# Two post-norm layers on one core: feature blocks through DRAM in whole rows, an expert tile in quarters, two evictions moved

## The chip, the core and the metric

The kernel runs on one core of a Trainium2 chip. The time is device microseconds of a whole execution: three runs gave 1348.04, 1350.30 and 1350.33 us, so the median is 1350.3 us. TensorE does matmuls and transposes, VectorE (DVE), ScalarE (ACT) and GpSimd (POOL) do the elementwise work, and SyncE (SP) issues most DMAs. Every engine runs its own list of instructions in order; semaphores tie the lists together.

## The reference, cut to what matters

```python
x = _layernorm(x + _L0_attn_ref(x, Wq, bq, Wk, bk, Wv, bv, gamma))      # layer A, attention
x = _layernorm(x + _L0_ffn_ref(x, gate_w, gate_b, expert_w, expert_b))  # 8 experts, gated
x = _layernorm(x + _L1_attn_ref(x, Wqkv, Wproj, bproj))                 # layer B, attention
x = _layernorm(x + _L1_ffn_ref(x, w_router, w_block))                   # top 75% of tokens

def _L1_attn_ref(x, Wqkv, Wproj, bproj):          # x: 8 batches of 1024 tokens, 256 features
    qkv = jnp.einsum('bnm,fm->bnf', x, Wqkv).reshape(b, n, 16, 48)
    q, k, v = (qkv[..., :16], qkv[..., 16:32], qkv[..., 32:])
    attn = jax.nn.softmax(jnp.einsum('bnhd,bngd->bnhg', q, k) / 8.0, axis=-1)
    out = jnp.einsum('bnhg,bngd->bnhd', attn, v).reshape(b, n, -1)
    return jnp.einsum('bni,mi->bnm', out, Wproj) + bproj
```

Layer B's attention is over the 16 heads of one token, not over tokens: for every token a 16 by 16 matrix of scores.

## The kernel before, in words

Each of the 8 batches goes through three stages: its layer-A attention, its experts, its layer-B attention with the last block. `turn(a, b, c)` interleaves three batches: attention A of `a`, experts of `b`, layer B of `c`. The order of each engine's instructions is written out by hand in that engine's `turn`; `closing` and `ending` do the same for the last two batches. The layer-B heads of a batch `c` are computed in six calls of `turn` and one of `closing`, seven places with the same order of work; those of the last batch come in `ending`, where little else is left to interleave.

**Through DRAM.** The projection to q, k and v gives six blocks of 128 features by 1024 tokens (`b_f`, feature tiles ft 0 to 5: two for q, two for k, two for v). Each is stored by one DMA of 512 KB to `scratch_qkv` from one of four slots (two halves of `stage`, `part`, and `flat_we` in the last batch), and a slot is written again only when its earlier store has landed. q, k and v are then read back in another layout, in which a partition holds one coordinate r (an eighth of the tokens) and one dimension d, and the heads and tokens run along the row: eight DMAs of 128 KB for each, one for each r, into 16 partitions each (`home_rows`), in pieces of 512 bytes. q and v go to `ct`, k to `keys`. In the last batch SP and ACT issue four q loads each, and SP five and POOL three k loads. The output of the heads is stored in the same manner (`o_store`, eight DMAs of 128 KB, four by SP in `b_loado` and four by ACT in `b_storeo`) and read back into `bt` by two DMAs of 512 KB.

**The heads.** `b_turnq` (ACT) and `b_turnv` (POOL, L705) re-order what was loaded: `blockdiag` is then built from it by the spreads. A spread is one instruction over 128 by 2048 fp16 elements that multiplies by a mask; DVE (L1554) and ACT (L873) share them. Eight DVE spreads make the first half of `blockdiag` for q, without which the score matmuls `S0` can't start. TensorE computes the scores in four blocks S0 to S3 (96 matmuls with 16 moving columns each), transposes the softmax (PT0 to PT3) and computes the outputs O0 to O3. These use two PSUM banks in turn: S3 waits until DVE has read S2, O0 until PT2 is read, O1 until PT3 is read, O2 until O0 is read. The outputs are evicted by ACT (high half) and DVE (low half) into `stage`, which held the turned v; so ACT's first output eviction waits for all v spreads.

**The experts.** An expert tile is 128 tokens; `a_moe(b, t)` on TensorE is four quarters of six matmuls, 128x512 each, one for each of four PSUM banks. DVE chains two quarters onto `x1`, ACT scales the other two into `part`, and POOL's `a_sum` adds them up (L670, L673, L677), reading two SBUF operands each. Tiles 1 to 7 are spread over the turn.

In POOL's list `b_turnv(c, 0)` stands right behind `a_sum(b, 0)` and ahead of `a_sum(b, 1)`. SP's `b_loadv` waits until both `b_turnq` are done, because v is loaded over q.

Of the kernel before, what the change touches and what calls it, by code (L numbers as in the profile page):

```python
# [5 lines left out]
def build_two_layer_postln(nc, x, wqk_t, bqk, wv, bv, gamma, gate_w, gate_b, expert_w, expert_b,  # L6
# [9 lines left out]
    NB, C, D = x.shape  # L16
# [28 lines left out]
    with ctx:  # L45
# [166 lines left out]
        k_rest = sem("k_rest")  # L212
# [10 lines left out]
        o_stored = sem("o_stored")  # L223
# [140 lines left out]
        K_SP = 5  # L364
# [20 lines left out]
        def o_store(r):  # L385

            return (scratch_o[:, :, r, :].rearrange("h d n -> d h n"),
                    ohl[DH * r:DH * (r + 1), :, :, :].rearrange("p h l n -> p h (l n)"))

# [6 lines left out]
        def home_rows(home, r):  # L396
            return home[DH * r:DH * (r + 1), :].rearrange("p (h n) -> p h n", h=H)
# [26 lines left out]
        class StepCount:  # L424
# [4 lines left out]
            def next(self, n):  # L429
# [8 lines left out]
        q_src, k_src, v_src = [scratch_qkv[D * n:D * (n + 1)].rearrange("(h d) (r n) -> h d r n", d=DH, r=T)  # L438
                               for n in range(3)]
# [19 lines left out]
        def _(sp):  # L459
# [33 lines left out]
            def b_f(b, k):  # L493
# [10 lines left out]
                sp.dma_start(scratch_qkv[P * ft:P * (ft + 1)], slots[s]).then_inc(stored[s], 16)  # L504

            def b_flast(b, ft):

                for k in range(12):
                    if f_tile(b, k)[0] == ft:
                        name = turn_of(b, f"F{k}")  # L510
                        sp.wait_ge(b_free[b_ring(name)], b_read(b, name))
                        sp.sem_inc(waits_held, 1)
                s = f_slot(b, ft)
                sp.dma_start(scratch_qkv[P * ft:P * (ft + 1)], slots[s]).then_inc(stored[s], 16)

            def b_loadq(b):
                for ft in (0, 1):
                    sp.wait_ge(*f_stored(b, ft))
                    sp.sem_inc(waits_held, 1)
                if b == NB - 1:  # L520
                    for r in range(T // 2):
                        sp.dma_start(home_rows(q_home(b), r), q_src[:, :, r, :].rearrange("h d n -> d h n"))\
                            .then_inc(q_loaded, 16)
                    return
                if later(b):
                    sp.wait_ge(ff_full, 4 * b)
                for r in range(T):
                    sp.dma_start(home_rows(q_home(b), r), q_src[:, :, r, :].rearrange("h d n -> d h n")).then_inc(q_loaded, 16)

            def b_loads(b):  # L530
                for ft in (0, 1, 3, 2):
                    b_flast(b, ft)
                b_loadq(b)
                b_loadk(b)
                sp.wait_ge(k_loaded, 16 * (T * b + K_SP))
                sp.sem_inc(waits_held, 1)
                sp.wait_ge(k_rest, 16 * (T - K_SP))
# [5 lines left out]
            def b_loadk(b):  # L543
                for ft in (2, 3):
                    sp.wait_ge(*f_stored(b, ft))
                    sp.sem_inc(waits_held, 1)
# [6 lines left out]

                for r in range(K_SP if b == NB - 1 else T):
                    sp.dma_start(keys[DH * r:DH * (r + 1), :, :],
                                 k_src[:, :, r, :].rearrange("h d n -> d h n")).then_inc(k_loaded, 16)

            def b_loadv(b):
                for ft in (4, 5):
                    sp.wait_ge(*f_stored(b, ft))  # L560
                    sp.sem_inc(waits_held, 1)
# [4 lines left out]
                for r in range(T):  # L566
                    sp.dma_start(home_rows(v_home(b), r), v_src[:, :, r, :]).then_inc(v_loaded, 16)

            def b_loado(b):
# [4 lines left out]
                for r in range(T // 2):  # L574
                    sp.dma_start(*o_store(r)).then_inc(o_stored, 16)
                sp.wait_ge(o_stored, 128 * (b + 1))
                sp.sem_inc(waits_held, 1)
# [1931 lines left out]
```

## Time and profile before

| | us |
|---|---|
| median of 3 runs | 1350.3 |
| profiled execution | 1349.4 |
| its span, first to last instruction | 1347.6 |
| TensorE busy | 1167.3 (87%) |
| DVE busy | 937.1 (70%) |
| ACT busy | 722.6 (54%) |
| POOL busy | 571.8 (42%) |
| mean granted TensorE clock | 0.891 |

Busy matmul time counts pipelined matmuls with modelled ends. A wait is shown as idle time before an instruction, in brackets, with what released it. "SPq" and "ACTq" are the sequencers that issue DMAs. Times in the timeline are counted from the first instruction.

### The profile page before, as it was taken

The numbers are of one execution on the slowest core, as the hardware profiler recorded it, in microseconds if no ns is written. First come the engines' busy times: TensorE is split into PE (matmuls) and PEld (weight loads), VectorE is DVE, ScalarE is ACT, GpSimd is POOL, SyncE is SP. The second block draws the span as 40 slices with busy tenths as digits, with TensorE's granted clock in tenths as the row PEclk, the third lists the DMA queues.
The fourth block names the chain that finished last, engine by engine and source line by source line (L and its number), as shares of the span: only waits on it lengthen the run. The fifth ranks groups of instructions, "written<-read, shape, count | busy, mean of one in ns | idle before, by whom it ended". The sixth has DMA issues, their size and how long they took to land.

```text
span 1347.6 us, 31178 instructions
## 1 busy us (share of the span) xinstructions
PE 1167.3 (87%) x12264; PEld 748.0 (56%) x12264; DVE 937.1 (70%) x2124; ACT 722.6 (54%) x1145; POOL 571.8 (42%) x882
## 2 busy tenths in 40 slices
PE   6688899998989999998999989898999988897464
PEld 4444466655665546655566556655566555654452
DVE  3544578677775868767775778668686777755866
ACT  3223375347753575547853477545754477544653
POOL 2235435335354355245354355354462352551124
PEclk8689898799979998799988999799987998799557
DMA  5000092203902075201902056021932029026430
GB/s 188 16 1 16 18 166 23 80 9 101 127 2 79 17 167 54 66 15 68 168 2 80 9 115 113 17 64 33 174 31 64 1 87 133 2 64 114 75 96 32
DMA packets 94009, 90.64 MB, mean 67 GB/s; under 512 B 7110, under 2 KB 83144, under 8 KB 93608
## 3 DMA queue, kind: packets, MB, share of 16 engines
q1 hardware_dynamic: 82008, 77.24, 29.3%
q0 software_dynamic: 2064, 6.69, 1.6%
q10 hardware_dynamic: 9792, 4.72, 1.4%
q8 instruction: 98, 1.61, 0.5%
q14 instruction: 47, 0.39, 0.1%
HBM read 46.68 MB, written 41.94 MB: 66 GB/s over the span
## 4 chain that ended last, share of the span: by engine, by line
PE 57%; DVE 18%; DMA 7%; issue 6%; ACT 5%; POOL 4%; ACTq 1%; SPq 1%; DVEq 0%; POOLq 0%
PE bank L1994 54%; DVE keys L1640 2%; DVE stats L1384 2%; DMA bt<-scratch_o 2%; DVE x L1525 2%; DVE gelu L1642 2%; POOL rs L655 2%; DMA scratch_o<-stage 2%; PE bank L2004 1%; ACT x L996 1%; DVE ct L1353 1%; DMA keys<-scratch_qkv 1%; ACTq L966 1%; ACT part L873 1%; DVE x L1708 1%
## 5 line engine op out<-in xcount | busy, mean ns | idle before, releaser
L1994 PE MATMUL bank<-we,at 128*128 128x512 f16 x1536 | 373.7, 403 | 1.9 <-DVE x L1525 1.9
L1994 PEld LDWEIGHTS bank<-we,at 128*128 128x128 f16 x1536 | 154.4, 102 | 194.6 <-issue 41.6
L670 POOL TENSOR_TENSOR part<-part 128x512 f32<-128x512 f32 x64 | 84.2, 1316 | 276.5 <-ACTq L1022 276.5
L873 ACT ACTIVATE part<-bank,wexp 128x256 f32<-128x256 f32 x256 | 104.3, 470 | 159.6 <-PE bank L1994 102.9
L1525 DVE SCALAR_TENSOR_TENSOR x<-bank,wexp,x 128x256 f32<-128x256 f32 x256 | 122.7, 479 | 53.0 <-PE bank L1994 46.5
L1994 PE MATMUL bank<-bt,wqkv 128*128 128x512 f16 x576 | 137.3, 380 | 20.8 <-DVE stage L1353 12.3
L996 ACT ACTIVATE x<-x,nm,rs 128x256 f32<-128x256 f32 x184 | 100.3, 593 | 69.3 <-POOL nm L658 68.1
L1353 DVE TENSOR_TENSOR stage<-bank,stage 128x512 f16<-128x512 f32 x110 | 74.4, 686 | 82.5 <-ACT stage L873 82.2
L651 POOL TENSOR_SCALAR nm<-mv 128x2 f32<-128x2 f32 x128 | 33.4, 261 | 207.1 <-DVE mv L1389 201.5
L1994 PE MATMUL bank<-keys,blockdiag 128*128 128x16 f16 x3072 | 97.5, 193 | 21.8 <-DVE blockdiag L1554 10.0
L1994 PEld LDWEIGHTS bank<-keys,blockdiag 128*128 128x128 f16 x3072 | 96.1, 103 | 26.4 <-issue 14.5
L873 ACT ACTIVATE stage<-bank 128x512 f16<-128x512 f32 x110 | 64.9, 597 | 77.2 <-PE bank L1994 75.5
L655 POOL TENSOR_TENSOR rs<-ve,half 128x2 f32<-128x2 f32 x128 | 96.0, 750 | 10.7
L1994 PEld LDWEIGHTS bank<-bt,wqkv 128*128 128x128 f16 x576 | 52.1, 97 | 86.1 <-DVE stage L1353 21.8
L2004 PE MATMUL bank<-const,x 128*128 128x128 f32 x384 | 59.4, 284 | 35.8 <-ACT x L996 25.5
L1994 PE MATMUL bank<-xs,blockdiag 128*128 128x16 f16 x2688 | 72.9, 173 | 16.8 <-issue 16.7
L1994 PEld LDWEIGHTS bank<-xs,blockdiag 128*128 128x128 f16 x2688 | 71.9, 102 | 18.9 <-issue 18.8
L873 ACT ACTIVATE blockdiag<-stage,const 128x2048 f16<-128x2048 f16 x40 | 78.1, 1993 | 0.0
L705 POOL COPY stage<-ct 128x2048 f16<-128x2048 f16 x14 | 54.2, 3871 | 49.4 <-DMA ct<-scratch_qkv 49.4
L1384 DVE BATCH_NORM_STATS2 stats<-x 128x6 f32<-128x256 f32 x184 | 68.9, 416 | 7.9 <-POOL x L677 4.4
L2004 PEld LDWEIGHTS bank<-const,x 128*128 128x128 f32 x384 | 45.5, 145 | 51.9 <-ACT x L996 33.2
L873 ACT ACTIVATE at<-bank 128x512 f16<-128x512 f32 x64 | 38.2, 596 | 62.4 <-PE bank L2004 60.9
(212 smaller groups left out, 2275.4 us busy)
## 6 DMA issues: line engine op xcount, KB each, us to landing
scratch_qkv<-stage SPq DMA_DIRECT2D x39, 512.0 KB, 3.3
ct<-scratch_qkv SPq DMA_DIRECT2D x112, 128.0 KB, 6.5
x_in<-in_x_dram SPq DMA_DIRECT2D x32, 256.0 KB, 2.7
bt<-scratch_o SPq DMA_DIRECT2D x16, 512.0 KB, 4.1
keys<-scratch_qkv SPq DMA_DIRECT2D x61, 128.0 KB, 6.0
out_dram<-x POOLq DMA_DIRECT2D x24, 256.0 KB, 2.7
scratch_qkv<-part SPq DMA_DIRECT2D x8, 512.0 KB, 7.8
scratch_o<-stage SPq DMA_DIRECT2D x32, 128.0 KB, 3.5
```

Of the source, the lines that this page charges most:

```text
L651: pool.tensor_scalar(nm[side][:, k, :], mv[side][:, k, :, 0], -1.0, None, ALU.mult)
L655: pool.tensor_tensor(rs[side][:, k, :], ve[side][:, k, :], half[:, 0:2], ALU.pow)\
L670: pool.tensor_tensor(part[:, 0:2, :], part[:, 0:2, :], part[:, 2:4, :], ALU.add)\
L705: pool.tensor_copy(v_rows[hf].rearrange("p (s c) h -> p s c h", c=8), turned(v_home(b), hf)).then_inc(v_turned[hf], 1)
L873: return act.activation(dst, src, ACT.Copy, scale=scale)
L996: ins = act.activation(dsts[t], srcs[t], ACT.Identity, bias=nm[side][:, k, t:t + 1], scale=rs[side][:, k, t:t + 1])
L1353: return dve.tensor_tensor(dst, src, hi, ALU.subtract)
L1384: ins = dve.bn_stats(stats[side][:, t, :], srcs[t])
L1525: ins = dve.scalar_tensor_tensor(out=dst, in0=m_bank[q][:, D * (e % 2):D * (e % 2 + 1)], scalar=wexp[:, t, e:e + 1], in1=dst, op0=ALU.mult ...
L1640: dve.tensor_scalar(beats_on(b)[:, o:o + P * (T - 1 - t)], scores_of(b)[:, P * (t + 1):C], me, None, ALU.is_le, ALU.add, accum_out=rowsum[ ...
L1994: ins = pe.matmul(dst, lhs, rhs, start=(n == 0), stop=(n == len(terms) - 1))
L2004: ins = pe.transpose(ps[:, 2 * P * k + P * t:2 * P * k + P * (t + 1)], src[:, 2 * p + t, P * k:P * (k + 1)], ident)
```

## The change

1. **Layout in DRAM.** The order of the features is permuted by the host in `Wqkv` (`by_dim` for q and k, `by_head` for v) and in `Wproj`, so that a block of 128 features holds, for each r, a whole row of each partition of the layout that is wanted. A block is now stored in pieces of 512 bytes (eight for each partition, `by_feature`) and loaded by one DMA of 512 KB with 4 KB for each of 128 partitions. So q, k and v take two loads each in place of eight, all issued by SP. The head outputs are stored by two DMAs of 512 KB in rows of 4 KB, and read back by two in pieces of 512 bytes; each read waits only for its own store. ACT issues no DMA any more, and POOL no k load.
2. **Order of the loads of the last batch.** The first q block is loaded before the store of block 2 is waited for; k's blocks are loaded 3 first.
3. **Expert tile 3 in quarters.** Its first quarter goes ahead of S3, two behind it, and the last between PT2 and PT3.
4. **ACT and DVE around the outputs.** Evictions O0 and O1 go ahead of ACT's part of expert tile 3. ACT's eviction of PT2 goes ahead of a layer-norm step. One v spread moves from ACT to DVE, which evicts PT2 before the first two spreads of half 1.

```diff
+        def half_of(home, ft):
+            return home[:, 2 * C * (ft % 2):2 * C * (ft % 2 + 1)]
+        def by_feature(memory):
+            return memory.rearrange("a m -> (a m)").rearrange("(r p n) -> p r n", r=T, p=P)
...
-                sp.dma_start(scratch_qkv[P * ft:P * (ft + 1)], slots[s]).then_inc(stored[s], 16)
+                sp.dma_start(by_feature(qkv_block(ft)), slots[s].rearrange("p (r n) -> p r n", r=T)).then_inc(stored[s], 16)
...
+            def load_block(b, ft, home, loaded):
+                sp.wait_ge(*f_stored(b, ft))
+                sp.sem_inc(waits_held, 1)
+                sp.dma_start(half_of(home, ft), qkv_block(ft)).then_inc(loaded, 16)
...
             def b_loads(b):
-                for ft in (0, 1, 3, 2):
+                for ft in (0, 1, 3):
                     b_flast(b, ft)
-                b_loadq(b)
+                load_block(b, 0, q_home(b), q_loaded)
+                b_flast(b, 2)
+                load_block(b, 1, q_home(b), q_loaded)
                 b_loadk(b)
...
             def b_loadv(b):
...
-                for r in range(T):
-                    sp.dma_start(home_rows(v_home(b), r), v_src[:, :, r, :]).then_inc(v_loaded, 16)
+                for ft in (4, 5):
+                    load_block(b, ft, v_home(b), v_loaded)
 
             def b_loado(b):
...
-                for r in range(T // 2):
-                    sp.dma_start(*o_store(r)).then_inc(o_stored, 16)
-                sp.wait_ge(o_stored, 128 * (b + 1))
-                sp.sem_inc(waits_held, 1)
                 for ht in range(KD):
-                    sp.dma_start(bt[:, ht, :, :].rearrange("p l n -> p (l n)"),
-                                 scratch_o[8 * ht:8 * ht + 8].rearrange("h d r n -> (h d) (r n)"))\
-                        .then_inc(o_loaded, 16)
+                    sp.dma_start(scratch_o[P * ht:P * (ht + 1)], ohl[:, 8 * ht:8 * ht + 8, :, :].rearrange("p h l n -> p (h l n)"))\
+                        .then_inc(o_stored[ht], 16)
+                for ht in range(KD):
+                    sp.wait_ge(o_stored[ht], 16 * (b + 1))
+                    sp.sem_inc(waits_held, 1)
+                    sp.dma_start(bt[:, ht, :, :].rearrange("p l n -> p (l n)").rearrange("p (r n) -> p r n", r=T),
+                                 by_feature(scratch_o[P * ht:P * (ht + 1)])).then_inc(o_loaded, 16)
...
             def turn(a, b, c):
...
-                    b_spreadv(c, 1, range(6, T))
-                if b is not None:
-                    a_moe(b, 3)
-                if c is not None:
+                    b_spreadv(c, 1, range(7, T))
                     b_o(c, 0)
                     b_o(c, 1)
+                if b is not None:
+                    a_moe(b, 3)
+                if c is not None:
                     b_o(c, 2)
                     b_o(c, 3)
```

On TensorE, the heads of one batch in a turn, from expert tile 1 to the output matmuls (`keys,blockdiag` is a score block, `const,prob` its transpose, `we,at` an expert tile, `xs,blockdiag` the outputs). Before:

```order
L1994 MATMUL bank<-we,at 128x512 x24
L1994 MATMUL bank<-keys,blockdiag 128x16 x192
L1994 MATMUL bank<-we,at 128x512 x24
L2169 MATMUL bank<-const,prob 128x128 x4
L1994 MATMUL bank<-keys,blockdiag 128x16 x96
L2169 MATMUL bank<-const,prob 128x128 x4
L1994 MATMUL bank<-keys,blockdiag 128x16 x96
L1994 MATMUL bank<-we,at 128x512 x24
L2169 MATMUL bank<-const,prob 128x128 x8
L1994 MATMUL bank<-xs,blockdiag 128x16 x384
```

And after, from the transposition PT0 on:

```order
L2128 MATMUL bank<-const,prob 128x128 x4
L1955 MATMUL bank<-keys,blockdiag 128x16 x96
L2128 MATMUL bank<-const,prob 128x128 x4
L1955 MATMUL bank<-we,at 128x512 x6
L1955 MATMUL bank<-keys,blockdiag 128x16 x96
L1955 MATMUL bank<-we,at 128x512 x12
L2128 MATMUL bank<-const,prob 128x128 x4
L1955 MATMUL bank<-we,at 128x512 x6
L2128 MATMUL bank<-const,prob 128x128 x4
L1955 MATMUL bank<-xs,blockdiag 128x16 x384
```

The 24 matmuls of expert tile 3 stood in one piece between S3 and PT2; six now stand ahead of S3, twelve behind it and six between the two transpositions.

On SP, the DMAs of one turn from the first stores of a batch on (`ct` takes q, later v). Before:

```order
L504 DMA scratch_qkv<-stage 128x2048 x3
L528 DMA ct<-scratch_qkv 16x16x256 x8
L504 DMA scratch_qkv<-part 128x2048
L504 DMA scratch_qkv<-stage 128x2048 x2
L555 DMA keys<-scratch_qkv 16x16x256 x8
L567 DMA ct<-scratch_qkv 16x16x256 x8
L575 DMA scratch_o<-stage 16x16x256 x4
L579 DMA bt<-scratch_o 128x2048 x2
L469 DMA x_in<-in_x_dram 128x2x256 x4
```

After:

```order
L503 DMA scratch_qkv<-stage 128x8x256 x3
L518 DMA ct<-scratch_qkv 128x2048 x2
L503 DMA scratch_qkv<-part 128x8x256
L503 DMA scratch_qkv<-stage 128x8x256 x2
L518 DMA keys<-scratch_qkv 128x2048 x2
L518 DMA ct<-scratch_qkv 128x2048 x2
L563 DMA scratch_o<-stage 128x2048 x2
L568 DMA bt<-scratch_o 128x8x256 x2
L468 DMA x_in<-in_x_dram 128x2x256 x4
```

The order is the same; twenty-four loads from `scratch_qkv` became six, over all 128 partitions each.

On ACT, from the end of the v spreads of half 0 to the output evictions (`xs<-bank` evicts a transposition, `blockdiag<-stage` is a spread, `x<-x,nm,rs` a layer-norm step, `part<-bank` the expert part, `stage<-bank` an output). Before:

```order
L873 ACTIVATE blockdiag<-stage,const 128x128x16 x2
L996 ACTIVATE x<-x,nm,rs 128x256 x2
L873 ACTIVATE xs<-bank 128x512 x2
L873 ACTIVATE blockdiag<-stage,const 128x128x16 x2
L873 ACTIVATE part<-bank,wexp 128x256 x4
L873 ACTIVATE stage<-bank 128x16x8x4 x4
L873 ACTIVATE at<-bank 128x2x256
L966 DMA scratch_o<-stage 16x16x256 x4
```

After:

```order
L851 ACTIVATE blockdiag<-stage,const 128x128x16 x2
L851 ACTIVATE xs<-bank 128x512
L967 ACTIVATE x<-x,nm,rs 128x256 x2
L851 ACTIVATE xs<-bank 128x512
L851 ACTIVATE blockdiag<-stage,const 128x128x16
L851 ACTIVATE stage<-bank 128x16x8x4 x2
L851 ACTIVATE part<-bank,wexp 128x256 x4
L851 ACTIVATE stage<-bank 128x16x8x4 x2
```

The expert part moved behind two output evictions, one spread left for DVE, and the four DMA issues are gone.

## Rows read from the trace of the kernel before

**Rows 1.** The page: TensorE's and other engines' busy time; the last chain.

```profile
PE 1167.3 (87%) x12264; PEld 748.0 (56%) x12264; DVE 937.1 (70%) x2124; ACT 722.6 (54%) x1145; POOL 571.8 (42%) x882
...
PE 57%; DVE 18%; DMA 7%; issue 6%; ACT 5%; POOL 4%; ACTq 1%; SPq 1%; DVEq 0%; POOLq 0%
```

**Rows 2.** Timeline, a turn: start us, us, engine, what, count, [idle before <-releaser].

```profile
508.79 6.34 SPq L567 DMA_DIRECT2D ct<-scratch_qkv  x8
...
510.13 7.36 DVE L1554 TENSOR_SCALAR blockdiag<-prob,const 128x2048 f16<-128x2048 f16 x8
...
513.24 1.05 POOL L677 TENSOR_TENSOR x<-x,part 128x256 f32<-128x256 f32 x1
...
517.41 2.73 DVE L1554 TENSOR_SCALAR blockdiag<-shared,const 128x2048 f16<-128x2048 f16 x4
...
518.54 4.59 PE L1994 MATMUL bank<-keys,blockdiag 128*128 128x16 f16 x144
...
522.53 3.74 POOL L705 COPY stage<-ct 128x2048 f16<-128x2048 f16 x1 [8.24 <-DMA ct<-scratch_qkv]
```

**Rows 3.** Timeline of the last such place, in closing.

```profile
1137.77 4.40 PE L1994 MATMUL bank<-keys,blockdiag 128*128 128x16 f16 x138 [0.92 <-issue]
```

**Rows 4.** By line, ns min/median/max: DVE's q spreads, POOL's v turns; timeline of one.

```profile
L1554 DVE TENSOR_SCALAR blockdiag<-prob,const x56: 737/744/1767, 198.0 to 1136.9; 128x2048 f16<-128x2048 f16 x56
...
L705 POOL COPY stage<-ct x14: 3735/3822/4436, 210.2 to 1151.2; 128x2048 f16<-128x2048 f16 x14
...
829.20 2.73 DVE L1554 TENSOR_SCALAR blockdiag<-shared,const 128x2048 f16<-128x2048 f16 x4
...
831.23 4.44 POOL L705 COPY stage<-ct 128x2048 f16<-128x2048 f16 x1 [5.15 <-DMA ct<-scratch_qkv]
```

**Rows 5.** DMA issues (count, KB, median us to landing); windows (last: DMA share, GB/s).

```profile
ct<-scratch_qkv SPq DMA_DIRECT2D x112, 128.0 KB, 6.5
...
bt<-scratch_o SPq DMA_DIRECT2D x16, 512.0 KB, 4.1
...
scratch_o<-stage SPq DMA_DIRECT2D x32, 128.0 KB, 3.5
...
510.20:513.00 2.80, 2.80 (x38) 2.51 (x35) 2.80 (x3) 2.48 (x3) 2.69 (x2) 1.00 1.28 118
...
570.00:573.00 3.00, 3.00 (x15) 1.17 (x13) 1.79 (x4) 0.84 (x2) 2.68 (x3) 1.00 0.94 340
```

**Rows 6.** Timeline, S3 to O3, PE, ACT and DVE apart; one window (PEclk 0.50).

```profile
537.26 3.04 PE L1994 MATMUL bank<-keys,blockdiag 128*128 128x16 f16 x96 [0.68 <-DVE prob L1588]
540.13 6.42 PE L1994 MATMUL bank<-we,at 128*128 128x512 f16 x24
...
548.49 5.03 PE L1994 MATMUL bank<-xs,blockdiag 128*128 128x16 f16 x192 [1.07 <-issue]
554.99 5.27 PE L1994 MATMUL bank<-xs,blockdiag 128*128 128x16 f16 x192 [1.47 <-issue]
...
551.83 1.54 ACT L873 ACTIVATE part<-bank,wexp 128x256 f32<-128x256 f32 x4
...
548.91 2.73 DVE L1554 TENSOR_SCALAR blockdiag<-stage,const 128x2048 f16<-128x2048 f16 x4
...
540.10:541.00 0.90, 0.90 (x10) 0.35 (x7) 0.67 (x1) 0.05 (x1) 0.62 (x1) 0.50 0.06 18
```

**Rows 7.** Waits: who, for whom, us in total, times, longest.

```profile
PE bank L1994 <- DMA bt<-scratch_o: 11.0, 5, 8.3
```

**Rows 8.** Timeline of the last batch: q, scores, v, outputs.

```profile
1243.82 2.42 DVE L1567 COPY we<-at 128x2048 f16<-128x2048 f16 x1 [3.97 <-DMA at<-scratch_qkv]
...
1251.92 4.26 PE L1994 MATMUL bank<-keys,blockdiag 128*128 128x16 f16 x134 [10.01 <-DVE blockdiag L1554]
...
1267.72 3.83 ACT L873 ACTIVATE stage<-xs 128x2048 f16<-128x2048 f16 x1 [4.69 <-DMA xs<-scratch_qkv]
...
1304.80 1.46 PE L1994 MATMUL bank<-wproj,bt 128*128 128x256 f16 x6 [8.33 <-DMA bt<-scratch_o]
```

## What the change was predicted to do

> **What bounds the kernel now.** First the page: TensorE is busy for 87% of the span and holds 57% of the chain that ended last, DVE 18% [rows 1]. So a microsecond by which TensorE's list is held up counts in full, and one saved elsewhere counts only where TensorE waits for it. Second, the timeline of one turn around the place where TensorE could start the scores: S0 starts at 518.54, straight behind expert tile 1, and the eight DVE spreads that it needs ended at 510.13 + 7.36 = 517.49 [rows 2]. That is a slack of 1.05 us, and the reader should keep it in mind. This place comes seven times with the same order, six in turns and one in closing, where TensorE already waits 0.92 us before S0 [rows 3]. Third, the same turn from S3 to O3, where TensorE waits 0.68, 1.07 and 1.47 us [rows 6]. Fourth, the last batch, where nothing covers its DMAs: TensorE waits 10.01 us ahead of S0 and 8.33 us ahead of the projection, ACT 4.69 us for v [rows 8].
>
> **Part 1, loads over 128 partitions.** Before, v is issued at 508.79 and POOL gets it at 522.5, after 8.24 us of waiting [rows 2]: 1 MB in eight DMAs into 16 partitions each, at 118 GB/s with the DMA share at 1.28. Two DMAs of 512 KB over 128 partitions are in the trace as the read of `bt`: 4.1 us to landing, and 340 GB/s in its stretch [rows 5]. By that row both v blocks have landed some 5 us after the issue, near 514. The Trainium skill explains the two rates (SBUF — State Buffer, "Door 1: The DMA port swizzle"): bandwidth depends on how many of 16 ports the partitions reach, and 16 neighbouring ones reach four. That changes no term here; it says that the row of `bt` is the one to go by.
>
> What does the early v buy? Nothing on TensorE, which doesn't wait for it, and it has a price. POOL's list has `b_turnv(c, 0)` right behind `a_sum(b, 0)`, which ends at 513.24 + 1.05 = 514.29 [rows 2]. So POOL starts its 3.74 us copy of v there, in the middle of the eight spreads, where it used to start behind all twelve. Do the two engines disturb each other? A spread takes 0.74 us at the median, but 1.77 at most [rows 4]; the slow ones lie beside `a_sum`, and so eight take 7.36 us where four others take 2.73 [rows 2]. The other way round, the copy that began at 831.23, while the last of four spreads from 829.20 was running, took 4.44 us where the shortest take 3.74, longer by what that spread still had to run, 0.70 [rows 4]. So they take turns. The nearest row for the sum: four spreads are done at about 514.8, POOL's copy then runs to 518.6, and the four that are left take 4 x 0.66 = 2.65, to 521.2. S0 starts at 521.3 in place of 518.54: **2.75 us lost in each of six turns**. In closing there is no slack, so the whole 3.74 is lost. Sum: 6 x 2.75 + 3.74 = **+20.2 us**. It doesn't matter when exactly v lands: any time up to the last of the eight spreads, 8.7 us after the issue, gives the same loss. Bounds: nothing (if the copy, which reads one operand, holds DVE back less than `a_sum` does) and 7 x 3.74 = 26. I take the value worked out, since 831.23 shows this very copy and this very spread exclude each other.
>
> By the Trainium skill (SBUF — State Buffer, "SBUF: two separate sides") DVE and GpSimd share one pair of SBUF ports, and whichever starts first keeps it for its whole instruction while the other stands still. By that rule the earlier v costs the 20 us above; if POOL merely waited for DVE and never the reverse, it would cost none. The rule speaks against the change, and the rows of the spreads and the copy agree with it.
>
> S1, tile 2 and PT0 are behind S0 on TensorE and move with it. DVE falls back by 3.7 us, but catches up: its reading of S0 and S1 had waits for ACT and TensorE between. q and k also land earlier, which nobody waits for in a turn.
>
> **Stores in 512-byte pieces.** No row shows a 512 KB store in such pieces. The nearest is the outputs' store, also in 512-byte pieces, 128 KB in 3.5 us; the nearest of the size is the read of `bt`, 512 KB in 4.1 us [rows 5]. So a store takes between about 4 us and, if four times the size took four times as long, 14. I take 4.5, nearer to the row of the size, because most of the 3.5 us for 128 KB must be latency. ACT's eviction F4 waits for the store of block 0, with several evictions and layer-norm steps of both engines between, which cover 4.5 us; near the upper end it would cost several microseconds a turn, and that counts under slower still.
>
> **Outputs through DRAM.** TensorE waits 11.0 us in five places for `bt`, 8.3 of them in the last batch [rows 7]; the other 2.7 lie in the turns. SP now issues two stores where eight on two queues were needed, and the first read waits for its own store alone. The read in 512-byte pieces lies between the 340 and the 118 GB/s of rows 5: 3.1 to 8.9 us for 1 MB; I take 4. That gives **-2.7 us**, bounded by 0 and, at 8.9, by 2 us lost in each turn.
>
> **Part 2, the last batch.** DVE waits 3.97 us for q before its 2.42 us turn, then spreads, and S0 follows at 1251.92 [rows 8]. With q over 128 partitions, two loads at the rate of `bt`, it lands before DVE is free at 1243.82 - 3.97 = 1239.85: S0 4.0 us sooner, and k isn't late either, with two loads in place of eight. v then no longer holds ACT for 4.69 us [rows 8]; behind it stands the exponential of score block 2, for which DVE waits; DVE has work of its own for about half of that time, so I count 2.1 more, an estimate. The fifth spread on DVE delays O2 by about 1.1 there. Behind the outputs ACT issues no DMAs ahead of its next step and the 8.33 us wait shrinks; DVE, still busy with the batch before, bounds the gain, and I take a quarter of the wait, 2.1. Sum: -4.0 - 2.1 + 1.1 - 2.1 = **-7.1 us**, bounds -10 and -3.
>
> **Parts 3 and 4.** The first quarter of tile 3 fills the 0.68 us ahead of S3. At PEclk 0.50, which is 1.2 GHz and what the stretch shows [rows 6], six matmuls of 512 columns take 2.56 us, at 2.4 GHz 1.28. So S3 ends 0.6 to 1.9 us later than before. From there DVE's list is the limit: it reads S3, spreads, reads PT2 and PT3 and spreads again, now five times in place of four (2.73 / 4 = +0.68). Against that, ACT's expert part of 1.54 us no longer stands ahead of the eviction of O0, which ends the 1.47 us wait ahead of O2 [rows 6]. Late 1.3 to 2.6, early 1.5 to 2: **0 us**, give or take 1 us in each of seven places.
>
> **Sum.** 1349.4 + 20.2 - 2.7 - 7.1 + 0 = 1359.8 for an execution like the profiled one; the median of the three runs lies 0.9 above that, so **1360.7**, or 0.8% slower.
>
> **Rivals.** *Faster: the copy doesn't hold DVE back* (or v lands after the last of the eight spreads, over 8.7 us from its issue). Then only the gains stay: 1350.3 - 9.8 = 1340.5, own range 1333 to 1348. For it: no row shows DVE's spread waiting for this copy, only the copy for the spread. Against it: the spreads beside `a_sum`. *Slower still: the clock or the 512-byte reads.* If most of tile 3 runs at 1.2 GHz once it is split by S3, PT3 comes 2 us late and O2 with it, 7 x 2 = 14 us on top: 1375. The same size comes if `bt` is read at 118 GB/s. For it: six matmuls at the low clock ahead of S3; against it: what clock there is afterwards comes back sooner too. *The change doesn't do what it says:* loads stay at 118 GB/s, because it is their pieces' source in DRAM and not the 16 partitions that limits them. Then no collision and little gain: 1349.
>
> **How the numbers follow.** The forecast has 0.67, the first rival 0.18, slower still 0.10, unchanged loads 0.05. About 0.2% (2.7 us) is what a measurement of this kernel can tell from no change. The forecast's own range, 1352 to 1369, comes from the bounds of parts 3 and 4 (7 us) and of the rest (3 us); a little of it lies within 0.2% or below. Faster: 0.17 + 0.03 = 0.20; same: 0.04 + 0.04 + 0.01 = 0.09; slower: 0.71. The range of 8 in 10 reaches from 1338, which takes in over half of the first rival, to 1370.
>
> **What would show it.** In the profile after: v landed some 5 us from its issue; POOL's copy starting right behind the first `a_sum`, one DVE spread of about 4.4 us in each turn, and S0 with 2.7 us of idle TensorE ahead of it, released by DVE. In the last batch, S0's wait near 6 us, and none of ACT for v. Ahead of O2 a wait near 1.5 us, released by ACT behind DVE's spreads. The prediction is wrong if spreads stay under 1.8 us, and then the time is near 1340.

## The result, and the profile after

The changed kernel takes **1357.9 us** at the median of seven runs (1353.3 to 1361.4); the kernel before took 1347.1 beside it. The ratio is 1.0072, with a 95% interval of 1.0053 to 1.0091: slower by 0.7%. Measured again (run e10 below) it was 1.0040, 1.0022 to 1.0057. The forecast was 1360.7 us and slower.

The page of the kernel after, as [rows 1]: busy time and the chain that ended last.

```profile
span 1359.6 us, 30973 instructions
...
PE 1169.8 (86%) x12264; PEld 750.2 (55%) x12264; DVE 977.3 (72%) x2132; ACT 707.0 (52%) x1137; POOL 577.5 (42%) x879
...
PE 54%; DVE 26%; issue 7%; ACT 6%; POOL 5%; DMA 2%; DVEq 0%; SPq 0%; POOLq 0%; ACTq 0%
```

Three things are to be seen. DVE's busy time grew by 40 us, though it got only one more spread a batch, 6 us in all; the rest is spreads that take longer, as shown below. Its share of the chain rose from 18% to 26%. The DMAs' share of the chain fell from 7% to 2%. The span less TensorE's busy time, the **idle time of TensorE**, was 1347.6 - 1167.3 = 180.3 us before and is 189.8 now, 9.5 more. I use this number for every run below, since it doesn't contain how fast the matmuls themselves ran. It is read from one execution of each kernel; the kernel after, profiled again, gave 187.8.

The same turn as in [rows 2], timeline of the kernel after:

```profile
515.93 1.39 SPq L518 DMA_DIRECT2D ct<-scratch_qkv  x2
517.24 10.86 DVE L1515 TENSOR_SCALAR blockdiag<-prob,const 128x2048 f16<-128x2048 f16 x8
520.33 1.05 POOL L666 TENSOR_TENSOR x<-x,part 128x256 f32<-128x256 f32 x1
521.58 3.97 POOL L694 COPY stage<-ct 128x2048 f16<-128x2048 f16 x1 [0.20 <-DMA ct<-scratch_qkv]
528.02 4.22 DVE L1515 TENSOR_SCALAR blockdiag<-shared,const 128x2048 f16<-128x2048 f16 x4
528.20 6.02 PE L1955 MATMUL bank<-keys,blockdiag 128*128 128x16 f16 x192 [2.39 <-issue]
```

POOL, done with the first sum at 521.38, waits 0.20 us for v and starts its copy at 521.58, 5.65 us after v's issue at 515.93 (before, it was 13.7 us). That is in the middle of the eight spreads. These take 10.86 us in place of 7.36, and S0 has 2.39 us of idle TensorE ahead of it. The profile names no releaser for that wait ("issue"), but the last of the eight spreads ends at 528.10, 0.10 before S0 starts. The wait is 2.39 or 2.40 us in each of the six turns. POOL's part of the next sum now lies beside the four spreads of half 1, which take 4.22 in place of 2.73; that was not in the prediction. All spreads of q, ns min/median/max, as in [rows 4]:

```profile
L1515 DVE TENSOR_SCALAR blockdiag<-prob,const x56: 740/1210/4257, 200.6 to 1154.9; 128x2048 f16<-128x2048 f16 x56
```

Seven of the 56, one in each place, take 4.2 us. Closing, to be read against [rows 3], and the last batch, against [rows 8]:

```profile
1143.75 5.35 PE L1955 MATMUL bank<-we,at 128*128 128x512 f16 x24 [1.88 <-DVE x L1486]
1144.88 11.27 DVE L1515 TENSOR_SCALAR blockdiag<-prob,const 128x2048 f16<-128x2048 f16 x8
1147.30 4.17 POOL L694 COPY stage<-ct 128x2048 f16<-128x2048 f16 x1
...
1156.25 3.93 PE L1955 MATMUL bank<-keys,blockdiag 128*128 128x16 f16 x123 [7.15 <-issue]
...
1256.61 2.47 DVE L1528 COPY we<-at 128x2048 f16<-128x2048 f16 x1
...
1264.60 6.02 PE L1955 MATMUL bank<-keys,blockdiag 128*128 128x16 f16 x192 [6.21 <-issue]
...
1275.76 3.81 ACT L851 ACTIVATE stage<-xs 128x2048 f16<-128x2048 f16 x1
...
1314.02 1.46 PE L1955 MATMUL bank<-wproj,bt 128*128 128x256 f16 x6 [6.23 <-DMA bt<-scratch_o]
```

DVE's turn of q has no wait any more (3.97 before), S0 waits 6.21 (10.01), ACT doesn't wait for v (4.69), the projection waits 6.23 (8.33). The projection's is now the only wait of TensorE for `bt`: those in the turns are gone. What closing shows is taken up in the part on why the prediction was right.

### The profile page after: what moved, and what is told of

Same layout as the page of the kernel before. It is cut to its first block, busy times and chain, and to the rows that moved or that the text cites. A ratio compares the mean times of both kernels' runs of the same rounds, so it can differ in the third digit from the quotient of the medians.

```text
span 1359.6 us, 30973 instructions
## 1 busy us (share of the span) xinstructions
PE 1169.8 (86%) x12264; PEld 750.2 (55%) x12264; DVE 977.3 (72%) x2132; ACT 707.0 (52%) x1137; POOL 577.5 (42%) x879
## 3 DMA queue, kind: packets, MB, share of 16 engines
q1 hardware_dynamic: 89544, 82.35, 19.2%
## 4 chain that ended last, share of the span: by engine, by line
PE 54%; DVE 26%; issue 7%; ACT 6%; POOL 5%; DMA 2%; DVEq 0%; SPq 0%; POOLq 0%; ACTq 0%
PE bank L1955 51%; DVE blockdiag L1515 5%; DVE x L1486 3%; DVE keys L1601 2%; DVE stats L1345 2%; PE bank L1965 2%; DVE gelu L1603 2%; POOL rs L644 2%; ACT x L967 1%; DVE ct L1314 1%; ACT part L851 1%; DVE x L1669 1%; DVE gt L1400 1%; DMA out_dram<-x 1%; DVE prob L1549 1%
## 5 line engine op out<-in xcount | busy, mean ns | idle before, releaser
L659 POOL TENSOR_TENSOR part<-part 128x512 f32<-128x512 f32 x64 | 87.5, 1367 | 297.0 <-ACTq L993 297.0
L926 ACT ACTIVATE prob<-prob 128x512 f32<-128x512 f32 x32 | 20.2, 630 | 130.0 <-DVE prob L1549 130.0
L700 POOL TENSOR_TENSOR prob<-prob,srec 128x512 f32<-128x512 f32 x32 | 36.6, 1144 | 99.8 <-DVE srec L1557 99.8
L1515 DVE TENSOR_SCALAR blockdiag<-prob,const 128x2048 f16<-128x2048 f16 x56 | 76.4, 1435 | 1.0
L1515 DVE TENSOR_SCALAR blockdiag<-stage,const 128x2048 f16<-128x2048 f16 x96 | 76.5, 845 | 0.0
```

The costliest lines, as they stand in the source:

```text
L659: pool.tensor_tensor(part[:, 0:2, :], part[:, 0:2, :], part[:, 2:4, :], ALU.add)\
L700: pool.tensor_tensor(pr, pr, srec[:, q % 2, :, None].broadcast_to([P, 32, H]), ALU.mult)\
L1515: ins = dve.tensor_scalar(blockdiag[:, dst_half, :, DH * r:DH * (r + 1)], rows, mask[:, r:r + 1], None, ALU.mult)
```

## Experiments

Each ratio is against the kernel before, run on the same chip beside it, with its 95% interval. "Idle" is TensorE's idle time in the profiled execution (180.3 before, 189.8 after).

| | ratio | idle, us |
|---|---|---|
| after | 1.0072 (1.0053 to 1.0091) | 189.8 |
| e10, after, measured again | 1.0040 (1.0022 to 1.0057) | 187.8 |
| e1, after, copy moved | 0.9883 (0.9858 to 0.9909) | 170.6 |
| e2, after, copy made twice | 1.0245 (1.0218 to 1.0272) | 221.5 |
| e3, layout alone | 1.0020 (1.0006 to 1.0034) | 189.6 |
| e4, layout alone, copy moved | 0.9869 (0.9844 to 0.9894) | 169.9 |
| e5, before, copy moved | 1.0007 (0.9976 to 1.0039) | 183.2 |
| e6, before, outputs alone | 0.9955 (0.9936 to 0.9974) | 177.6 |
| e7, e1 without quarters | 0.9894 (0.9863 to 0.9924) | 169.8 |
| e8, e1 without part 4 | 0.9912 (0.9883 to 0.9940) | 175.4 |
| e9, after, copy waits for 8 spreads | 1.0030 (1.0013 to 1.0047) | 183.7 |
| e11, after without quarters | 1.0036 (1.0014 to 1.0059) | 189.5 |
| e12, before, with a collision put in | 1.0262 (1.0229 to 1.0295) | 216.2 |

### e1 and e2: take the cause away, double it

e1, in POOL's `turn` and `closing` (the `if` lines of `turn` are left out):

```diff
                 a_sum(b, 0)
-                b_turnv(c, 0)
                 a_sum(b, 1)
+                b_turnv(c, 0)
```

> The kernel after, with POOL's copy of v for half 0 moved behind the sum of expert tile 1 (in the turn and in closing), so that it can't start before TensorE has done that tile. Theory (the copy stands between DVE's eight spreads and holds up S0): the 2.4 us of idle TensorE ahead of S0 is gone in six turns (14.4 us), and closing gets 3.7 back, so 1357.9 - 18 = about 1340 us, no DVE spread over 1.8 us. Rival 1 (the wait ahead of S0 is made up for later, since DVE and ACT bound the stretch behind it): the gap goes, but it comes back ahead of S2, PT0 or S3, and the time is 1350 to 1358. Rival 2 (the loss against the kernel before comes from the stores and reads in 512-byte pieces or from the order of expert tile 3): 1358 us.

Measured: 1335.7 us, 1.17% below the kernel before, some 4 us less than expected. The theory holds: TensorE's idle time fell by 189.8 - 170.6 = 19.2 us, and the longest DVE spread of q takes 1.77 us. e1's turn, timeline:

```profile
508.67 7.36 DVE L1514 TENSOR_SCALAR blockdiag<-prob,const 128x2048 f16<-128x2048 f16 x8
...
517.08 6.06 PE L1954 MATMUL bank<-keys,blockdiag 128*128 128x16 f16 x192
...
521.51 0.69 DVE L1548 TENSOR_TENSOR prob<-bank,smax 128x512 f32<-128x512 f32 x1
521.72 3.75 POOL L694 COPY stage<-ct 128x2048 f16<-128x2048 f16 x1
...
522.90 0.69 DVE L1554 TENSOR_REDUCE ssum<-prob 128x32 f32<-128x512 f32 x1 [0.70 <-ACT prob L925]
...
525.94 0.69 DVE L1554 TENSOR_REDUCE ssum<-prob 128x32 f32<-128x512 f32 x1 [0.70 <-ACT prob L925]
```

The eight spreads take 7.36 us again, as before, and no wait stands ahead of S0 in any of the six turns. The copy, from 521.72 to 525.47, now lies beside DVE's softmax in f32, and there nobody is held: the copy takes 3.75 us, and the same sum over `prob` takes 0.69 beside the copy (at 522.90) and after its end (at 525.94). So it is not "POOL beside DVE" that costs, but POOL beside the fp16 spreads. By the Trainium skill (SBUF — State Buffer, "SBUF: two separate sides") only certain DVE instructions take the pair of ports that DVE shares with GpSimd: those in a 2-port perf mode, and those with two SBUF inputs while GpSimd reads SBUF too. The rows agree in so far as the spreads are held and these f32 steps are not; which mode an instruction runs in, they don't show.

e2, in `b_turnv`:

```diff
+                if hf == 0:
+                    pool.tensor_copy(v_rows[hf].rearrange("p (s c) h -> p s c h", c=8),
+                                     turned(v_home(b), hf)).then_inc(v_again, 1)
+                    pool.wait_ge(v_again, b + 1)
                 pool.tensor_copy(v_rows[hf].rearrange("p (s c) h -> p s c h", c=8),
                                  turned(v_home(b), hf)).then_inc(v_turned[hf], 1)
```

> The kernel after, with POOL's copy of v for half 0 made twice in a row at the same place (the same data, so the result is unchanged). Theory: the second copy also gets between the eight spreads, and costs S0 another 3.7 us in each of seven places, 26 us, so about 1384 us, with two DVE spreads of over 4 us in each turn or one of 8. Rival 1: DVE gets all of its spreads done between the two copies, or only one copy can catch it: 1358 to 1362 us. Rival 2, the copy doesn't matter: 1358 us.

Measured: 1382.1 us, 24 more than the kernel after; expected 26. That the two numbers are so near is in part chance: the idle time grew by 31.7 us, not 26, and TensorE's busy time in the profiled execution was 11.3 us shorter (1158.5 against 1169.8), for which I have no reason. Timeline of e2 (from the third spread on):

```profile
524.84 13.38 DVE L1520 TENSOR_SCALAR blockdiag<-prob,const 128x2048 f16<-128x2048 f16 x6
...
526.59 4.24 POOL L696 COPY stage<-ct 128x2048 f16<-128x2048 f16 x1
530.88 3.99 POOL L699 COPY stage<-ct 128x2048 f16<-128x2048 f16 x1
...
538.32 5.98 PE L1960 MATMUL bank<-keys,blockdiag 128*128 128x16 f16 x192 [7.27 <-issue]
```

S0's wait grew from 2.39 to 7.27 us. Both copies get in between, with spreads between them: two of the eight take over 4 us here (4.27 and 4.12).

### e3 to e6: the layout, with and without the collision

e3 undoes parts 3 and 4; e4 is e3 with e1's edit. The diff shows TensorE's list and the main lines of ACT's; the `if` lines, and the order around PT2 on ACT and DVE, are left out.

```diff
-                    a_moe(b, 3, (0,))
                     b_s(c, 3)
-                    a_moe(b, 3, (1, 2))
+                    a_moe(b, 3)
                     b_pt(c, 2)
-                    a_moe(b, 3, (3,))
                     b_pt(c, 3)
...
-                    b_spreadv(c, 1, range(7, T))
-                    b_o(c, 0)
-                    b_o(c, 1)
+                    b_spreadv(c, 1, range(6, T))
                     a_moe(b, 3)
+                    b_o(c, 0)
+                    b_o(c, 1)
```

> The kernel after with parts 3 and 4 undone: expert tile 3 in one piece behind S3, ACT's expert part ahead of the output evictions, its layer-norm step ahead of PT2, six spreads of half 1 on DVE and two on ACT. What is left is the layout in DRAM and the order of loads. Theory (parts 3 and 4 cancel out): 1358 us, within 3. Rival (splitting tile 3 costs the time, since its first quarter runs at 1.2 GHz ahead of S3): 1347 to 1352. Rival (parts 3 and 4 gain what the collision would lose, up to 1.5 us in seven places): 1365 to 1368.

> The same kernel without parts 3 and 4, with POOL's copy behind the sum of expert tile 1 as well. Theory: 18 us less than that kernel, about 1340, and thus 7 us faster than before, because the last batch keeps its gain (S0's wait 6 us in place of 10) and the wait for bt in the turns is gone. Rival (the layout itself brings nothing but the collision): 1347. Beside the run with parts 3 and 4 and the copy moved it shows again what these parts are worth: theory 0 within 3 us.

Measured: 1352.8 and 1332.6 us. Both are faster than expected, e3 by 5 us (outside its "within 3") and e4 by about 7. The difference, 20.2 us, is the collision in the layout alone, where 18 were expected and the prediction had 20.2. Its idle time says the same: 189.6 - 169.9 = 19.7. Without the collision the layout gains 1.3%, 17.4 us, more than the 9.8 to 11 of the prediction. The profiles say what of it is which: page of e4,

```profile
span 1332.1 us, 30973 instructions
...
PE 1162.2 (87%) x12264; PEld 747.0 (56%) x12264; DVE 934.4 (70%) x2124; ACT 723.9 (54%) x1145; POOL 570.9 (43%) x879
```

TensorE's idle time fell by 10.4 us, near what the prediction's waits add up to without the fifth spread (2.7 + 4.0 + 2.1 + 2.1 = 10.9). The other 5.1 us are in TensorE's busy time: the same 12264 matmuls took 1162.2 us in place of 1167.3. The prediction had no term for that. The mean granted clock (0.895 in e4, 0.891 before) doesn't account for it by itself: e3 has the lowest of the three, 0.886, and a busy time of 1160.9. Why the matmuls took less stays open.

Is moving the copy a gain of its own? e5 makes e1's edit in the kernel before.

> The kernel before, with the one edit that POOL's copy of v for half 0 stands behind the sum of expert tile 1. It tells whether the 17 to 20 us that moving the copy gave back in the changed layout come from the collision alone. Theory: before, the copy starts at 522.53, behind all twelve spreads, so there is no collision to remove; POOL's sum of tile 1 only comes 3.7 us sooner, and the time stays at 1350, within 3. Rival (moving the copy is a gain of its own, since the sum of tile 1 frees its buffer for ACT sooner): 1340 to 1345, and then the layout's own gain is 8 to 12 us and not 17.

Measured: a ratio of 1.0007, and by its interval a gain of at most some 3 us. There was no collision to remove. So the 20 us between e3 and e4 are the collision's.

e6 is the kernel before with the outputs' part alone (two stores by SP, two reads, each behind its own store; `Wproj` permuted):

```diff
-                for r in range(T // 2):
-                    sp.dma_start(*o_store(r)).then_inc(o_stored, 16)
-                sp.wait_ge(o_stored, 128 * (b + 1))
                 for ht in range(KD):
+                    sp.dma_start(scratch_o[P * ht:P * (ht + 1)], ohl[:, 8 * ht:8 * ht + 8, :, :].rearrange("p h l n -> p (h l n)"))\
+                        .then_inc(o_stored[ht], 16)
...
-                b_storeo(c)
```

> The kernel before, with the outputs' part of the change alone: two stores of 512 KB in rows of 4 KB by SP, two reads in pieces of 512 bytes, each behind its own store, no DMA on ACT. As predicted: 2.7 us of waits for bt in the turns go and 2.1 in the last batch, so 1350 - 4.8 = 1345. Rival 1 (the outputs are the larger part of the layout's 17 us, because ACT no longer spends time on issues in each turn): 1338 to 1342. Rival 2 (the reads in 512-byte pieces are as slow as the stores are faster): 1350.

Measured: 0.9955, 6.1 us (3.5 to 8.6), expected 4.8. Waits of e6's TensorE (us, times, longest), to be read against [rows 7]:

```profile
PE bank L1994 <- DMA bt<-scratch_o: 6.3, 1, 6.3
```

11.0 us in five places became 6.3 in one: 2.7 in the turns and 2.0 in the last batch, where the prediction had 2.7 and 2.1. The reads in 512-byte pieces cost little (4.1 us to landing before), and the stores in such pieces took 3.5 us where 4.5 had been assumed. Page of the kernel after, DMAs with KB each and us to landing:

```profile
scratch_qkv<-stage SPq DMA_DIRECT2D x39, 512.0 KB, 3.5
...
bt<-scratch_o SPq DMA_DIRECT2D x16, 512.0 KB, 4.7
```

### e7, e8, e10, e11: parts 3 and 4

e7 is e1 with `a_moe(b, 3)` in one piece behind S3; e8 is e1 with part 4 undone.

> The kernel after with the copy moved, and with expert tile 3 in one piece behind S3 again (part 3 undone, part 4 kept). Theory (part 3 is worth 0): the same as with it, 1333 to 1336. Rival (the quarter ahead of S3 makes PT2 and with it O0 late, and costs 0.3 to 0.5 us in seven places): 1331 to 1333, faster than both the versions with and without parts 3 and 4.

> The kernel after with the copy moved and with part 4 undone (ACT's expert part ahead of the output evictions, its layer-norm step ahead of PT2, six spreads of half 1 on DVE), part 3 kept. Theory (both parts are worth 0 each): 1333 to 1336. Rival (the evictions gain up to 1.5 us in seven places and the quarters lose as much): then this one is the slowest of the four versions with the copy moved, 1340 to 1345.

Measured: 1332.4 and 1335.2 us. The four versions with the copy moved have ratios of 0.9869 (neither part), 0.9894 (part 4), 0.9912 (part 3) and 0.9883 (both), each give or take 0.003. Only the widest gap, e4 to e8, lies at the edge of what these intervals resolve. The idle times (169.9, 169.8, 175.4, 170.6) say that the quarters alone (e8) cost 5 us and that the evictions' order gives these back, and the traces show where, ahead of the first output block O0. e8, a turn:

```profile
550.72 5.26 PE L1952 MATMUL bank<-xs,blockdiag 128*128 128x16 f16 x192 [2.77 <-issue]
```

This wait is 2.77 us in five of e8's seven places and 1.75 in two. It is 1.02 in all seven of e7, where tile 3 is in one piece, and mostly 1.79 in e1, which has both parts. Against that, the quarters end TensorE's wait ahead of S3, which is 1.13 us in five of e7's seven places and 0.70 in two. So this is e8's rival, at about half the size: part of what the quarters lose, the evictions give back.

e10 is the kernel after again, and e11 the kernel after with the quarters undone.

> The kernel after, unchanged, on the same chip as the two beside it, since the experiments so far lay 5 us apart by the way they were paired: with the copy at its early place the version without parts 3 and 4 measured 1.0020 of before and the whole change 1.0072, while with the copy moved the two measured 0.9869 and 0.9883. Theory (parts 3 and 4 cost nothing and the 5 us are the spread of the clock between executions): 1.002 to 1.005 of before. Rival (with the collision there, parts 3 and 4 do cost 5 us): 1.007 again.

> The kernel after with part 3 undone alone (expert tile 3 in one piece behind S3), and the collision left in. If the quarters cost 5 us where the collision is: 1.002 of before, like the version without parts 3 and 4. If nothing does: the same as the whole change within 3 us. If it is part 4 that costs: 1.007.

Measured: 1.0040 and 1.0036. The quarters cost nothing that can be seen. Against e3's 1.0020, parts 3 and 4 together come to 2.7 us by this pairing (about 0 to 6 by the intervals), and to 7 by the first. It isn't waiting: the idle times of e3, the kernel after, e10 and e11 are 189.6, 189.8, 187.8 and 189.5 us. It is TensorE's busy time: 1160.9, 1169.8, 1171.2 and 1168.9 us. How much of that is the clock stays open: the seven executions of the kernel after go from 1353.3 us at a mean granted clock of 0.893 to 1361.4 at 0.881. The profiled one is the longest of them, and its windows show a stretch near the end (third column from the right is PEclk):

```profile
1327.00:1332.00 5.00, 3.34 (x16) 2.52 (x15) 0.94 (x2) 2.56 (x6) 0.58 (x2) 0.50 0.01 2
1332.00:1337.00 5.00, 5.00 (x13) 1.51 (x10) 1.60 (x5) 1.19 (x2) 3.09 (x5) 0.51 0.00 0
```

Ten microseconds were granted 1.2 GHz there. The work from the projection to the end took 1359.6 - 1314.0 = 45.6 us, and 1332.1 - 1290.7 = 41.4 in e4, whose list is the same there. The copy isn't the reason: e1, with the copy moved, took 45.7 there, and e2, with it doubled, 41.0.

### e9: leave the order, delay the copy

```diff
                 pool.wait_ge(v_loaded, 32 * (b + 1))
+                if hf == 0 and b < NB - 1:
+                    pool.wait_ge(q_spread[0], b + 1)
```

> The kernel after with nothing moved: POOL's copy of v for half 0 stays between the sums of tiles 0 and 1, but it now also waits until DVE has made the eight spreads of half 0 (in the turns and in closing; the last batch's copy is on DVE). Theory: S0 no longer stands behind the copy; the copy meets the four spreads of half 1, which have slack ahead of S2, and one of these is the long one. 1358 - 20 to 25 = 1333 to 1338, the same as with the copy moved behind the sum of tile 1. Rival (the gain of the moved copy came from the order of the sums and not from the time at which the copy starts; or the longer h1 spreads now hold up S2): 1345 to 1358.

Measured: 1355.1 us, a ratio of 1.0030, against 1.0040 of the kernel after beside it; 1333 to 1338 had been expected. **My theory of the place failed here**, and the second half of the rival holds, with a different victim. Timeline of e9:

```profile
514.86 7.35 DVE L1517 TENSOR_SCALAR blockdiag<-prob,const 128x2048 f16<-128x2048 f16 x8
...
522.13 7.83 DVE L1517 TENSOR_SCALAR blockdiag<-shared,const 128x2048 f16<-128x2048 f16 x4
522.37 4.21 POOL L696 COPY stage<-ct 128x2048 f16<-128x2048 f16 x1 [3.36 <-DVE blockdiag L1517]
523.27 6.07 PE L1957 MATMUL bank<-keys,blockdiag 128*128 128x16 f16 x192
...
529.88 2.03 DVE L1488 SCALAR_TENSOR_TENSOR x<-bank,wexp,x 128x256 f32<-128x256 f32 x4
530.93 7.54 PE L1957 MATMUL bank<-we,at 128*128 128x512 f16 x24 [1.59 <-DVE x L1488]
```

The eight spreads are undisturbed and S0 doesn't wait. But now the four behind them take 7.83 us in place of 2.73 (all twelve take 15.2 us, as they take 15.1 in the kernel after and 10.1 in the kernel before), and DVE's part of expert tile 1, which stands behind all twelve, comes late. TensorE waits 1.59 us for its banks ahead of expert tile 2, and S2 doesn't suffer. Over the run TensorE waits 14.0 us for that line, where the kernels before and after wait 1.9:

```profile
PE bank L1957 <- DVE x L1488: 14.0, 8, 2.6
```

These 12.1 us are most of the 13.1 by which e9's idle time is above e1's. So it is DVE's whole list from the spreads to expert tile 1 that has no room for the copy, and not the first eight spreads alone.

### e12: put the cause into the kernel before

```diff
+                if hf == 0 and b < NB - 1:
+                    pool.wait_ge(k_loaded, 16 * T * (b + 1))
+                    for ft in (2, 3, 4, 5):
+                        pool.wait_ge(*f_stored(b, ft))
+                    pool.tensor_copy(v_rows[0].rearrange("p (s c) h -> p s c h", c=8),
+                                     turned(beats_keys, 0)).then_inc(k_again, 1)
+                    pool.wait_ge(k_again, b + 1)
                 pool.wait_ge(v_loaded, 16 * T * (b + 1))
```

> The kernel before, with its layout and its order, and with one more copy on POOL in each of the seven places: while POOL waits for v (8.24 us there), it makes the same copy from the loaded keys into the place that v will get, and then the real one over it. So the collision is put into the kernel before, and nothing else is changed. Theory (a 3.74 us copy that starts behind the first sum, while DVE makes its twelve spreads, costs TensorE 2.4 to 3.7 us a time, by itself): 1350 + 17 to 24 = 1367 to 1374, with one DVE spread of 4.2 us in each place. Rival (it takes the new layout's earlier loads, or the stores by 512-byte pieces, for the loss to appear): 1350 to 1355. Where DVE's whole list of spreads and the expert part behind them is the limit, and not the first eight spreads alone, as the run with POOL waiting for the eight spreads suggested, the loss is nearer to 24 than to 17.

Measured: 1386.4 us, 35 more than the kernel before (31 to 40). That the cause is enough without the new layout is shown; the size is one and a half to two times the forecast of 17 to 24. Timeline of e12:

```profile
520.17 10.86 DVE L1562 TENSOR_SCALAR blockdiag<-prob,const 128x2048 f16<-128x2048 f16 x8
...
524.27 4.21 POOL L708 COPY stage<-keys 128x2048 f16<-128x2048 f16 x1
...
530.95 6.31 DVE L1562 TENSOR_SCALAR blockdiag<-shared,const 128x2048 f16<-128x2048 f16 x4
531.13 6.03 PE L2002 MATMUL bank<-keys,blockdiag 128*128 128x16 f16 x192 [2.39 <-issue]
532.42 4.29 POOL L713 COPY stage<-ct 128x2048 f16<-128x2048 f16 x1 [3.94 <-DMA ct<-scratch_qkv]
...
538.23 6.98 PE L2002 MATMUL bank<-we,at 128*128 128x512 f16 x24 [1.07 <-DVE x L1533]
```

The added copy does just what the early v does after the change: 10.86 us for eight spreads, 2.39 ahead of S0. But it pushed the spreads back by 3.5 us, and so the real copy, which used to find them done, now meets the last four (6.31 us). That is e9's collision on top of the first. Over the run TensorE waits 15.1 us for DVE's part of the experts, 13.2 more than in the kernel before.

## Why the prediction was right

**The collision, +20.2 us: right, in mechanism, place and size.** Its signs are in the trace: the landing, the copy's start, the long spread, the wait of 2.39 us where 2.75 were worked out. Only the releaser that was forecast for that wait, DVE, isn't named by the profile. The waits ahead of S0 add up to 6 x 2.39 + 4.93 = 19.3 us (4.93 for closing, see below), and the idle time of e1 is 19.2 below that of the kernel after. e3 and e4 measure the collision at 20.2 us by their medians. (The 0.66 us for a spread in the prediction's sum stands in no row: four took 2.73, or 0.68 each, which moves the wait by 0.1.) In the whole change the medians of the kernel after and of e1, each as a ratio to before, lie 21 (by e10) to 26 us apart. The rival "the copy doesn't hold DVE back" is excluded, as is "loads not faster".

**One sentence of it was wrong.** "DVE falls back by 3.7 us, but catches up", because of the waits in its reading of S0 and S1. e9 shows that it doesn't: ahead of those waits stands DVE's part of expert tile 1, and TensorE's tile 2 waits for it. It made no difference to the sum, because the lateness of S0 covered it. But the same sentence led me to expect in e9 that a later copy would be free, and that was 17 to 22 us off. The advice that it implies (delay the copy past the eight spreads) would have been wrong; delaying it past TensorE's tile 1, as e1 does, is right. Also the limit in the first rival, v landing after the last of the eight spreads, was drawn too early: e9's copy starts there and still costs, with a ratio of 1.0030 to the kernel before against e1's 0.9883.

**Closing: a price of 3.7 us predicted, 4.9 measured.** TensorE waits 7.15 us ahead of S0 there, against 0.92 + 3.74 = 4.66 predicted. Before, in closing:

```profile
1130.20 6.64 PE L1994 MATMUL bank<-we,at 128*128 128x512 f16 x24 [1.88 <-DVE x L1525]
...
1131.33 6.33 DVE L1554 TENSOR_SCALAR blockdiag<-prob,const 128x2048 f16<-128x2048 f16 x8
```

The eight spreads took 6.33 us before and take 11.27 now, 4.94 more. The other 1.3 us are expert tile 1, which took 6.64 us in this execution of the kernel before and takes 5.35 now, so that TensorE comes to the wait earlier. e1, without the collision and with 5.35 for the tile, waits 2.22, and 7.15 - 2.22 = 4.93. The 0.92 of [rows 3] was thus low by what a slower tile 1 hid of the wait.

**Outputs and last batch, -9.8 us together: right in the waits, too small in the time.** Turns: 2.7 predicted, 2.7 measured. S0's wait in the last batch fell by 3.8 where 4.0 were forecast. From that S0 to the projection it took 1304.80 - 1251.92 = 52.9 us before and 1314.02 - 1264.60 = 49.4 after, 3.5 less, where the three terms for v, the fifth spread and `bt` came to -2.1 + 1.1 - 2.1 = -3.1. `bt` alone gave the 2.1 that were forecast, but between 1.4 and 2.5 in the other runs with the new outputs (waits of 7.0 us in e1 and 5.8 in e9). ACT doesn't wait for v. The term that was missing is TensorE's busy time, put at no change: without the collision it fell by 5.1 us (e4), and the layout's gain was 17.4 us by the median where I had about 10.

**Parts 3 and 4, 0 us within 7: right in the sum, not in its parts.** The first quarter of tile 3 took 2.77 us for six matmuls, at a granted clock of 0.52 in the window from 544.90 to 547.40, where 2.56 were forecast:

```profile
545.03 2.77 PE L1955 MATMUL bank<-we,at 128*128 128x512 f16 x6
...
557.86 5.22 PE L1955 MATMUL bank<-xs,blockdiag 128*128 128x16 f16 x192 [1.79 <-issue]
...
564.53 3.88 PE L1955 MATMUL bank<-xs,blockdiag 128*128 128x16 f16 x139 [1.45 <-issue]
```

But the 1.5 to 2 us that the evictions' order was to bring by ending the wait ahead of O2 didn't come there: that wait is 1.45 us, and it was 1.47 [rows 6]. Its staying near 1.5 is no sign of a gain. What moved is the wait ahead of O0, from 1.07 us to 1.79 in this turn, and that ahead of S3, which is gone; e8 shows that without the evictions' order O0 would wait 2.77. In waiting the two parts cancel out, as forecast. Whether they cost TensorE up to 7 us of busy time together with the collision stays open.

**The number itself is in part luck.** The predicted terms add up to 20.2 - 2.7 - 7.1 = 10.4 us of waiting, and TensorE's idle time grew by 9.5. But the forecast of 1360.7 came so near 1357.9 also because two misses offset each other: the layout gained some 7 us more than forecast (e4), and the kernel after is 3 to 7 us slower than e3, where parts 3 and 4 stood at 0.

**A better version.** e4 (layout alone, copy behind the sum of tile 1) is 1.3% faster than the kernel before and 1.7 to 2.0% faster than the kernel after. e1 and e7 can't be told from it.

## What to carry to other kernels

A transfer that nobody on the critical path waits for can still be the gate that keeps a GpSimd instruction away from DVE's fast fp16 work. Before a load is made faster, look up which instruction it releases, where in time that will now run, and what DVE does there. If the two meet, try to reorder the GpSimd list so that the copy falls beside DVE's f32 or PSUM work, as e1 does; a wait that only shifted it to the next piece of fp16 work (e9) gained nothing that could be measured here.

## What the runs showed of the hardware

- A 128x2048 fp16 copy on POOL and a DVE spread of 128x2048 fp16 exclude each other in both directions: the spread that meets the copy takes 4.2 us in place of 0.74, while the copy's own 3.74 us become 3.85 to 4.43, longer by less than one spread (kernel after, e2, e9, e12). Eight spreads in a row don't keep the copy out. Beside DVE steps in f32 that read a PSUM bank or sum in SBUF, the same copy takes 3.75 us and the steps 0.69, as without it (e1).
- Storing 512 KB in pieces of 512 bytes over all 128 partitions took 3.5 us to landing, where the same blocks in whole rows took 3.3 in the kernel before; reading 512 KB into such pieces took 4.7 us where whole rows took 4.1. So pieces of 512 bytes alone aren't what made the loads before slow (6.5 us for 128 KB); that leaves the 16 partitions of each and their number, which no run changed apart from the pieces.
